# First attention's queries and output in three tiles per four heads, and the background dequantisation ending where the second layer's attention begins

## The reference

```
_L0_xattn(latents, context):             # H, KV, HD = 16, 4, 96; G = H // KV = 4 heads per key/value head
    hidden = concatenate([context, latents], axis=1)          # 64 + 256 keys
    q = (latents @ Wq.T)                                      # 16 heads of 96
    k, v = hidden @ Wk.T, hidden @ Wv.T                       # 4 heads of 96
    scores = einsum('bkgqd,bksd->bkgqs', q, k) / sqrt(96)
    out = einsum('bkgqs,bksd->bkgqd', softmax(scores), v)
    return out.reshape(b, q_len, H * HD) @ Wo.T

_L3_ffn(x, w1, w2, w3):                  # each weight is first rounded to a 16-value code
    absmax = max(abs(flat.reshape(-1, 64)), axis=1)
    dq = CODE[searchsorted(bounds, flat / absmax)] * absmax
    return (silu(x @ dq1.T) * (x @ dq2.T)) @ dq3.T

x = x + _L0_xattn(_layernorm(x), ctx, ...);  x = x + _L0_ffn(...)      # layer 0
x = x + _L1_xattn(_layernorm(x), ctx);       x = x + _L1_ffn(...)      # layer 1
x = x + _L2_xattn(...);                      x = x + _L2_ffn(...)      # layer 2
x = x + _L3_xattn(...);                      x = x + _L3_ffn(_layernorm(x), L3_w1, L3_w2, L3_w3)
```

## Time and profile before

| what | value |
|---|---|
| times of the three runs | 1754.61, 1754.72, 1748.97 us, median 1754.61 |
| the profiled execution: its time, its span | 1750.64 us, 1748.9 us |
| PE, DVE, ACT, POOL busy | 1451.7, 1115.7, 461.4, 312.8 us |
| mean granted TensorE clock | 0.884 of full |
| layer 0's attention (first transposes of the probabilities to last `pv0`) | 68 to 616 us |
| its feed-forward | to 873 us |
| layer 1; layer 2 up to `gate2` | to 1047 us; to 1139 us |

### The profile page before, as it was taken

How to read it: one execution, slowest core, us unless ns; L and a number is a source line. 1 busy time by engine, 2 the same in 40 slices (tenths; PEclk the granted TensorE clock), 3 DMA queues, 4 the chain that set the end, 5 groups by cost and what they waited for, 6 DMA issues and landing times.

```text
span 1748.9 us, 19188 instructions
## 1 busy us (share of the span) xinstructions
PE 1451.7 (83%) x6585; PEld 1150.0 (66%) x6585; DVE 1115.7 (64%) x2569; ACT 461.4 (26%) x994; POOL 312.8 (18%) x186
## 2 busy tenths in 40 slices
PE   6559999998999889898377878589997566589998
PEld 5347776685776668686266767487886355477786
DVE  4567777768777658767967556634466788854142
ACT  3214423423334323232212113113213222122010
POOL 4101211211112112111121013116422421012120
PEclk9779999999999999899655897569998788799999
DMA  6421331322223221321011013001111000001011
GB/s 202 139 69 51 89 88 49 93 77 64 77 67 84 64 62 42 84 82 41 24 43 40 23 49 91 17 1 36 46 52 49 25 1 1 1 24 61 13 38 48
DMA packets 99409, 96.42 MB, mean 55 GB/s; under 512 B 13138, under 2 KB 72418, under 8 KB 99314
## 3 DMA queue, kind: packets, MB, share of 16 engines
q1 hardware_dynamic: 98802, 94.35, 18.3%
q0 software_dynamic: 512, 0.85, 0.2%
HBM read 84.34 MB, written 10.82 MB: 54 GB/s over the span
## 4 chain that ended last, share of the span: by engine, by line
PE 62%; DVE 26%; ACT 4%; issue 4%; DMA 2%; SPq 1%; POOL 1%; ACTq 0%; DVEq 0%; POOLq 0%
PE bank L1651 49%; PE bank L1991 5%; PE bank L1743 4%; DVE nf_y L1595 3%; DVE st L1136 2%; DVE xn L1154 1%; PE bank L1676 1%; DVE mx L1504 1%; DVE xT L1113 1%; DVE e L1518 1%; PE bank L1733 1%; DVE sm L1516 1%; DVE mx L1187 1%; PE bank L1947 1%; DMA nf_a<-in_L_w 1%
## 5 line engine op out<-in xcount | busy, mean ns | idle before, releaser
L1651 PE MATMUL bank<-xT,slots 128*128 128x512 f32 (+1 forms) x1920 | 471.2, 404 | 10.4 <-DVE xT L1113 6.9
L1651 PEld LDWEIGHTS bank<-xT,slots 128*128 128x128 f32 (+1 forms) x1920 | 357.1, 187 | 110.9 <-issue 10.2
L808 POOL TENSOR_TENSOR slots<-staging,slots 128x1024 fp32r<-128x1024 f32 (+4 forms) x97 | 230.2, 2376 | 1107.0 <-ACT slots L896 1106.9
L1595 DVE TENSOR_SCALAR nf_y<-nf_w 128x512 fp32r<-128x512 f32 (+2 forms) x495 | 233.6, 499 | 25.7 <-PE bank L1991 24.7
L1651 PE MATMUL bank<-slots,h 128*128 128x512 f32 (+1 forms) x728 | 181.7, 410 | 20.1 <-DVE h L1243 13.9
L1651 PEld LDWEIGHTS bank<-slots,h 128*128 128x128 f32 (+1 forms) x728 | 142.9, 197 | 56.8 <-DVE h L1243 14.8
L1991 PE MATMUL bank<-nf_y,nf_d 128*128 128x512 f32 (+2 forms) x495 | 169.7, 427 | 10.7 <-DVE nf_y L1595 8.5
L896 ACT ACTIVATE slots<-staging 128x1024 fp32r<-128x1024 f32 (+4 forms) x97 | 98.2, 1018 | 189.9 <-PE bank L1651 173.6
L929 ACT ACTIVATE e<-bank,mx 128x320 f32<-128x320 f32 x128 | 66.4, 524 | 272.2 <-DVE mx L1190 268.1
L1209 DVE TENSOR_TENSOR x<-bank,x 128x512 f32<-128x512 f32 x72 | 49.7, 690 | 125.7 <-PE bank L1651 125.6
L1991 PEld LDWEIGHTS bank<-nf_y,nf_d 128*128 128x128 f32 (+1 forms) x495 | 94.9, 197 | 46.9 <-issue 15.6
(11 more groups left out here) (244 smaller groups left out, 1905.0 us busy)
## 6 DMA issues: line engine op xcount, KB each, us to landing
staging<-in_L_wqkT SPq DMA_DIRECT2D x16, 480.0 KB, 3.7
nf_out<-nf_w SPq DMA_DIRECT2D x30, 256.0 KB, 2.1
staging<-nf_out SPq DMA_DIRECT2D x30, 256.0 KB, 2.8
staging<-in_L_woT SPq DMA_DIRECT2D x16, 384.0 KB, 3.3
staging<-in_L_w SPq DMA_DIRECT2D x12, 512.0 KB, 3.9
nf_a<-nf_max SPq DMA_DIRECT2D x40, 128.0 KB, 3.5
nf_r<-nf_rcp SPq DMA_DIRECT2D x40, 128.0 KB, 3.4
nf_w<-in_L_w SPq DMA_DIRECT2D x15, 256.0 KB, 4.2
```

What stands on the lines that cost most here:

```text
L808: g.tensor_tensor(lo, split_source(i), hi.bitcast(FP32), ALU.subtract).then_inc(*sig.mark("weight_low", i))
L1595: v.tensor_scalar(nf_y[0:rows, i % STAIR_RING, 0:size], w_, bound, first, compare, ALU.mult)\
L1651: ins = mm(dst, l_, r_, start=i == 0, stop=i == len(passes) - 1)
```

## The change

`q0` of a stage is made in three tiles of 128 columns in place of four of 96. Tile j holds head j in rows 0 to 95 and a third of the fourth head in rows 96 to 127; the query weights are laid out for that on the host. ACT and DVE copy each tile in two pieces: head j in place, and the 32 rows of the fourth head to rows 32j of the fourth column block (`spare(j)`), where `scores0` reads it as before. `pv0` of the first three heads is unchanged. That of the fourth writes three pieces of 32 rows back to rows 96 to 127 of the three tiles. So `o0` contracts three full tiles of 128 rows, with Wo's rows in that order, in 9 matmuls. Its second weight chunk is half as long. WEIGHT of `q0` goes from 2.6 to 3.5, with three steps in place of four. BACKGROUND_END moves from `gate2` to `scores1`: all of the dequantisation lies in layer 0.

```diff
-BACKGROUND_END = "gate2"
+BACKGROUND_END = "scores1"
...
+QT0, SPARE0 = HPG * HD0 // P, P - HD0
+def spare(j):
+    return slice(j * SPARE0, (j + 1) * SPARE0)
...
-                steps += [("q0", s + 1, h) for h in ((0, 1), (2,), (3,))[j - 5]]
+                steps.append(("q0", s + 1, j - 5))
...
-WEIGHT = {"v0": 1.9, "k0": 2.6, "kc0": .7, "q0": 2.6, "scores0": .9, ...
+WEIGHT = {"v0": 1.9, "k0": 2.6, "kc0": .7, "q0": 3.5, "scores0": .9, ...
...
-        q0 = sb("q0", [HD0, 2, 2, HPG, HALF], F32R, s0)
+        q0 = sb("q0", [P, 2, 2, HPG, HALF], F32R, s0)
...
+            for i, n in enumerate((2, 1)):
+                rows = a["L0_woT"][(s % G0 * QT0 + 2 * i) * P:(s % G0 * QT0 + 2 * i + n) * P]
+                chunk(("o0", s, i), P, (n, D), [((slice(None),), rows.rearrange("(h p) n -> p h n", p=P))])
... ScalarE
-            def q0_(s, h):
-                high("q0", (s, h), q0[:, s % 2, 0, h], psum(("q0", s, h))[0:HD0])
+            def q0_(s, j):
+                bank = psum(("q0", s, j))
+                act.wait_ge(*sig.when("q0_product", (s, j)))
+                sc.activation(q0[0:HD0, s % 2, 0, j], bank[0:HD0], ACT.Copy)
+                sc.activation(q0[spare(j), s % 2, 0, QT0], bank[HD0:P], ACT.Copy).then_inc(*sig.mark("q0_high", (s, j)))
...
-                high("pv0", n, q0[:, s % 2, 0, h, bl * S:(bl + 1) * S], psum(("pv0", n))[0:HD0, 0:S])
+                if h < QT0:
+                    high("pv0", n, q0[0:HD0, s % 2, 0, h, cs], bank[0:HD0, 0:S])
+                    return
+                act.wait_ge(*sig.when("pv0_product", n))
+                for j in range(QT0):
+                    ins = sc.activation(q0[HD0:P, s % 2, 0, j, cs], bank[spare(j), 0:S], ACT.Copy)
+                ins.then_inc(*sig.mark("pv0_high", n))
... VectorE
-                low("q0", (s, h), q0[:, s % 2, 1, h], psum(("q0", s, h))[0:HD0], q0[:, s % 2, 0, h])
+                dve.wait_ge(*sig.when("q0_high", (s, j)))
+                v.tensor_tensor(q0[0:HD0, s % 2, 1, j], bank[0:HD0], q0[0:HD0, s % 2, 0, j].bitcast(FP32), ALU.subtract)
+                low("q0", (s, j), q0[spare(j), s % 2, 1, QT0], bank[HD0:P], q0[spare(j), s % 2, 0, QT0])
...
+                dve.wait_ge(*sig.when("pv0_high", n))
+                for j in range(QT0):
+                    ins = v.tensor_tensor(q0[HD0:P, s % 2, 1, j, cs], bank[spare(j), 0:S],
+                                          q0[HD0:P, s % 2, 0, j, cs].bitcast(FP32), ALU.subtract)
+                ins.then_inc(*sig.mark("pv0_low", n))
... TensorE
-                qk(s, ("q0_product", (s, h)), h * HD0, (h + 1) * HD0, lambda k: xt(k, hf * HALF, (hf + 1) * HALF), bank[0:HD0])
+                qk(s, ("q0_product", (s, j)), j * P, (j + 1) * P, lambda k: xt(k, hf * HALF, (hf + 1) * HALF), bank[:])
...
-                pe.wait_ge(*sig.when("q0_low", (s, h)))
+                pe.wait_ge(*sig.when("q0_low", (s, min(h, QT0 - 1))))
...
-                pairs = [([q0[:, s % 2, p, h, i * P:(i + 1) * P] for p in range(2)], [w[h // 2][p][:, h % 2] for p in range(2)])
-                         for h in range(HPG)]
+                pairs = [([q0[:, s % 2, p, j, i * P:(i + 1) * P] for p in range(2)], [w[j // 2][p][:, j % 2] for p in range(2)])
+                         for j in range(QT0)]
```

More of the change, by code:

```diff
@@ L109, in schedule @@
     steps += [("v0", 0, i) for i in range(TPH + BPH)]
-    steps += [("k0", 0), ("kc0", 0)] + [("q0", 0, h) for h in range(HPG)]
+    steps += [("k0", 0), ("kc0", 0)] + [("q0", 0, j) for j in range(QT0)]
     units = [(s, bl, h) for s in range(2 * G0) for h in range(HPG) for bl in range(BPH)]
@@ L235, in schedule @@
     return steps
-WEIGHT = {"v0": 1.9, "k0": 2.6, "kc0": .7, "q0": 2.6, "scores0": .9, "turn0": .4, "pv0": 1, "o0": 2.6, "up0": 2.6,
+WEIGHT = {"v0": 1.9, "k0": 2.6, "kc0": .7, "q0": 3.5, "scores0": .9, "turn0": .4, "pv0": 1, "o0": 2.6, "up0": 2.6,
           "down0": 4.8, "scores1": 2, "pv1": 1.6, "route1": 1, "z1": 2.6, "zt1": .5, "b1": 2.6, "k2": 1.3, "m2": 1.3,
@@ L493, in o0_chunks @@
         def o0_chunks(s):
-            for i in range(2):
-                rows = a["L0_woT"][(s % G0 * HPG + 2 * i) * HD0:(s % G0 * HPG + 2 * i + 2) * HD0]
-                chunk(("o0", s, i), HD0, (2, D), [((slice(None),), rows.rearrange("(h p) n -> p h n", p=HD0))])
+            for i, n in enumerate((2, 1)):
+                rows = a["L0_woT"][(s % G0 * QT0 + 2 * i) * P:(s % G0 * QT0 + 2 * i + n) * P]
+                chunk(("o0", s, i), P, (n, D), [((slice(None),), rows.rearrange("(h p) n -> p h n", p=P))])
         v0_chunks(0)
@@ L942, in pv0 @@
             def pv0(n, s, bl, h):
-                high("pv0", n, q0[:, s % 2, 0, h, bl * S:(bl + 1) * S], psum(("pv0", n))[0:HD0, 0:S])
+                cs, bank = slice(bl * S, (bl + 1) * S), psum(("pv0", n))
+                if h < QT0:
[5 more added lines that the diff above has]
+                ins.then_inc(*sig.mark("pv0_high", n))
             def up0(f, hf):
@@ L1200, in pv0 @@
             def pv0(n, s, bl, h):
-                cs = slice(bl * S, (bl + 1) * S)
-                low("pv0", n, q0[:, s % 2, 1, h, cs], psum(("pv0", n))[0:HD0, 0:S], q0[:, s % 2, 0, h, cs])
+                cs, bank = slice(bl * S, (bl + 1) * S), psum(("pv0", n))
+                if h < QT0:
+                    low("pv0", n, q0[0:HD0, s % 2, 1, h, cs], bank[0:HD0, 0:S], q0[0:HD0, s % 2, 0, h, cs])
+                    return
+                dve.wait_ge(*sig.when("pv0_high", n))
[3 more added lines that the diff above has]
+                ins.then_inc(*sig.mark("pv0_low", n))
             def add_to_x(stage, key, t, src, name=None, mark=None, scale=None):
@@ L1710, in kc0_, with q0_ @@
                    lambda k: [ctxT[:, q, k, hf * n:(hf + 1) * n] for q in range(2)], bank[0:HD0, 0:n])
-            def q0_(s, h):
+            def q0_(s, j):
                 hf = s // G0
-                bank = claim(("q0", s, h), ("q0_low", (s, h)))
-                qk(s, ("q0_product", (s, h)), h * HD0, (h + 1) * HD0, lambda k: xt(k, hf * HALF, (hf + 1) * HALF), bank[0:HD0])
+                bank = claim(("q0", s, j), ("q0_low", (s, j)))
+                qk(s, ("q0_product", (s, j)), j * P, (j + 1) * P, lambda k: xt(k, hf * HALF, (hf + 1) * HALF), bank[:])
             def scores0(n, s, bl, h):
-                pe.wait_ge(*sig.when("q0_low", (s, h)))
+                pe.wait_ge(*sig.when("q0_low", (s, min(h, QT0 - 1))))
                 pe.wait_ge(*sig.when("k0_low", s))
@@ L1722, in scores0 @@
                     bank = claim(("scores0", n, i), ("exp0", (n, i)))
-                    l_ = [q0[:, s % 2, p, h, bl * S + i * P:bl * S + (i + 1) * P] for p in range(2)]
+                    l_ = [q0[0:HD0, s % 2, p, h, bl * S + i * P:bl * S + (i + 1) * P] for p in range(2)]
                     product(bank[:, 0:KEYS0], [(l_, [k0[:, s % 2, p, bl] for p in range(2)])])\
@@ L2032, in lay_out @@
     rows = [((c * HPC + h) // REP3) * HD3 + j for c in range(KT) for h in range(HPC) for j in range(HD3)]
+    tiles = np.array([[h * HD0 + d for d in range(HD0)] + [QT0 * HD0 + h * SPARE0 + d for d in range(SPARE0)]
+                      for h in range(QT0)]).reshape(-1)
+    heads = np.concatenate([g * HPG * HD0 + tiles for g in range(G0)])
     return {
@@ L2036, in lay_out @@
         "ctxT": t(d["ctx_4096"].reshape(B * CTX, D).T),
-        "L0_wqkT": t(np.stack([np.concatenate([wq[g * HPG * HD0:(g + 1) * HPG * HD0], wk[g * HD0:(g + 1) * HD0]]).T
+        "L0_wqkT": t(np.stack([np.concatenate([wq[g * HPG * HD0 + tiles], wk[g * HD0:(g + 1) * HD0]]).T
                                for g in range(G0)])),
         "L0_wvT": t(d["L0_xattn_Wv"].T),
-        "L0_woT": t(d["L0_xattn_Wo"].T),
+        "L0_woT": t(d["L0_xattn_Wo"].T[heads]),
         "L0_wgT": t(d["L0_ffn_w_gate"].T), "L0_wuT": t(d["L0_ffn_w_up"].T), "L0_wdT": t(d["L0_ffn_w_down"].T),
```

## The result

The changed kernel takes 1779.5 us (median of 4 runs, 1777.4 to 1780.7), the kernel before 1754.7 (4 runs, 1749.0 to 1759.4): ratio 1.014, 95% interval 1.011 to 1.017. It is slower by 25 us. Its profiled span is 1775.6 us against 1748.9.

The account below looks back on a forecast made before the run. PE was taken to bound the attention, and neither PE nor DVE to fill layers 1 and 2. Attention -12, feed-forward +9, layers 1 and 2 -28 sum to -31 on 1750.6 us: 1719.5, median forecast 1720, range 1692 to 1748.

Parts of the forecast that it names:

- I take +17 us: Attention: PE's idle time grows by 17 us, from half of the late items' 30 us and the fourth heads' pieces.
- -28.9 of PE work: Attention: removed `q0` and `o0` matmuls, 22.3 us each, less 15.7 us for 67 added sums, net -28.9 us.
- the items' 30 us: Attention: nine m = 2 items each late by 3 to 4 us more, some 30 us of DVE, half under queued products.
- a few tenths for each fourth head: Attention: a few tenths of a us of PE idle time for each of 16 fourth heads.
- forecast 44.6: PE products: 8 `q0` products removed, 22.3 us, and 96 matmuls of `o0`, 22.3 us.
- +65 forecast: Attention: DVE's work grows by 65 us: `q0` subtractions 10.9, `pv0` pieces 13.5, 67 dequantisation steps 40.7.
- up to 9 us of shorter locks: `o0`'s half-length second chunk shortens POOL's lock on DVE; up to 9 us come back, left out of the sum.
- +9 forecast: Feed-forward: 3.3 us for 14 more sums and 6 us for a late m = 2 item, together +9 us.
- -28 forecast: Layers 1 and 2: all 81 dequantisation steps leave, 35 us of the chain; four fifths taken, -28 us.
- Rival (d): Layers 1 and 2: without filler sums PE's clock stays at its lower level, +30 us, 1750, no change; chance 0.09.
- Rival (c): Attention: DVE becomes the bound, unit 9.5 us instead of 8.57, +60 there, +41 in all, 1792; chance 0.07.
- (b): Attention: idle time grows by the whole 29 us and eats the gain; -12 in all, about 1739; chance 0.14.

Follow-up runs that it names:

- e6: The changed kernel with an m = 2 item's maxima and reciprocals loaded by one DMA each instead of ten (wrong rows): 1755.9 us, ratio 1.0018.
- e5: e1 from the third stage on without the fourth head's query copies and with one of its three output pieces: 1737.8 us, ratio 0.9911.
- e9: e6 from the third stage on without the fourth head's query copies and two of its three output pieces: 1720.5 us, ratio 0.9841.
- e13: e10 from the third stage on without DVE's 32-row query pieces and two of its three output pieces, ACT's kept: 1732.5 us, ratio 0.9891.
- e14: e10 with ACT's pieces left out in the same places as DVE's in e13, and DVE's kept: 1730.4 us, ratio 0.9879.
- e10: The changed kernel with right tables in 11 DMA issues per m = 2 item instead of 21, and sums five steps behind: 1741.8 us, ratio 0.9953.
- e1: The changed kernel with the dequantisation again spread up to `gate2` (tiles alone): 1759.1 us, ratio 1.0049.
- e7: e2 with its m = 2 items loaded by 3 DMAs instead of 21 (wrong rows): 1750.6 us, ratio 0.9990.
- e12: The kernel before with dequantisation ending at `scores1`, 11 DMA issues per m = 2 item and sums five steps behind: 1748.6 us, ratio 0.9989.
- e15: e10 with only the queries in three tiles, the outputs in four heads as before: 1761.6 us, ratio 1.0051.
- e16: e10 with only the outputs in three tiles, the queries in four heads as before: 1742.3 us, ratio 0.9939.
- e2: The kernel before with only the dequantisation's end moved to `scores1`: 1791.7 us, ratio 1.0231.
- e17: e15 without ACT's and DVE's 32-row pieces of the queries from the third stage on: 1748.7 us, ratio 0.9986.

## Why the prediction was wrong

The step that failed is "I take +17 us" for the growth of PE's idle time in the attention, with the -28.9 of PE work beside it. Their sum, -12, came out as +51.

- **Idle time.** +49 instead of +17. The mechanisms named (ACT ahead of DVE, late m = 2 items, waits of 3 to 7 us) were the right ones; the runs price the items at 24 us in after (e6) and the pieces at 21 to 35 (e5, e9), with what the clock adds to both. I had spread the items' 30 us over PE's queue by half, and given the pieces a few tenths for each fourth head. I also gave ACT's 21.5 us no term but those tenths, and asked only whether DVE's sum passes PE's. It didn't, and each us on ACT or DVE still cost 0.4 to 0.8 us (e13 and e14 against e10, e5 against e1, e9 against e6).
- **PE work.** -28.9 was forecast, +2.8 measured. The products gave 40.4 us in a stretch that holds 39.1 of the forecast 44.6, so that price was right. The sums cost 31.5 instead of 15.7: 0.235 us is a sum in a run of six, while over the attention they average 0.336 before and 0.361 after. Another 12 us are mostly untouched forms that ran slower at a mean clock of 0.91 instead of 0.95, a term that the sum did not have. The tiles alone bring that clock too (e1), and cheaper loads give a part of it back (e6, e7).
- **DVE's work.** +65 forecast, +46.5 measured. A 32-row piece costs what a 96-row one does (below), as taken. The added steps were cheaper: POOL is busy 9.1 us less in the attention, and a step lasts 506 ns in the mean against 530, 180 to 600 us:
```profile
L1621 DVE TENSOR_SCALAR nf_y<-nf_w 128x512 fp32r<-128x512 f32 x295 | 139.5, 506 | 3.6 <-PE bank L2017 2.4
```
   That is the term left out, up to 9 us of shorter locks. The Trainium skill (SBUF — State Buffer, "Who interferes with whom") says that DVE in its 2-port modes and GpSimd block each other for a whole instruction. The rows agree, and the packings one by one show that the shorter chunk goes with it. These are the same steps, 180 to 600 us, in e12 (no packing), e15 (queries, full chunk) and e16 (outputs, shorter chunk):
```profile
L1596 DVE TENSOR_SCALAR nf_y<-nf_w 128x512 fp32r<-128x512 f32 x313 | 155.3, 528 | 10.4 <-PE bank L1992 9.7
```
```profile
L1622 DVE TENSOR_SCALAR nf_y<-nf_w 128x512 fp32r<-128x512 f32 x304 | 148.8, 522 | 11.4 <-PE bank L2018 10.4
```
```profile
L1616 DVE TENSOR_SCALAR nf_y<-nf_w 128x512 fp32r<-128x512 f32 x320 | 152.4, 509 | 5.3 <-PE bank L2012 4.1
```
- **Feed-forward.** +9 forecast, +7 measured. e6 with its cheap loads is 5 us shorter there, near the 6 that were put for the late item.
- **Layers 1 and 2.** -28 forecast, -29 measured, clock 0.68, forecast "near 0.70". Rival (d) did not happen there: of the 35 us that the steps held of the chain, 29 came back. e2 and e7 won back 28 and 27 us there too.
- **The rivals.** Rival (c) put the unit at 9.5 us and the whole at 1792; the unit came to 9.77. But its mechanism is not what happened: it has DVE as the bound, and DVE was busy 308.7 of 420 us, as before. Engines that wait for each other gave the length that a full one would have. (b) was the gain given back; it was given back with more.
- **What the forecast time needs.** e9 came to 1720.5, the forecast to half a us, but not by its terms: the attention +1 instead of -12, the feed-forward 0 instead of +9, layers 1 and 2 -28, and 3.5 less behind them. That agreement is luck. The tiles' gain there just pays for the 65 steps moved in, which alone lengthen the attention by 23 us in e7 (0.35 each) and bring back 27 in layers 1 and 2: the move was worth next to nothing even with cheap loads.

What stays open: why queries' tiles gain nothing without their pieces (e17), and why the tiles alone lower the clock of the attention to 0.91 (e1), which only 24 us more of idle time go with.

## What to carry to other kernels

When work moves from the engine that bounds to others that feed it step by step, add it along the relay (copy, subtraction, step, sum), not engine by engine: room in the totals is no cover. Before packing steps more densely, look at the longest transfer chain between two of them and at how long its issue takes on its queue; here an edit of three lines that halves the issues was worth 26 us, as much as the change had lost. Price a filler instruction by its mean in the stretch where it will stand, not by the best run of it.

## What the runs showed of the hardware

Copies and subtractions by form in after (min/median/max ns):
```profile
L892 ACT ACTIVATE q<-bank x72: 364/374/598, 87.2 to 1563.2; 96x256 fp32r<-96x256 f32 x48, 128x256 fp32r<-128x256 f32 x16, 128x512 fp32r<-128x512 f32 x8
L959 ACT ACTIVATE q<-bank x48: 371/372/375, 149.5 to 668.2; 32x256 fp32r<-32x256 f32 x48
L1226 DVE TENSOR_TENSOR q<-bank,q x48: 416/420/425, 150.7 to 669.5; 32x256 fp32r<-32x256 f32 x48
L930 ACT ACTIVATE q<-bank x24: 588/594/597, 38.8 to 596.6; 96x512 fp32r<-96x512 f32 x24
L931 ACT ACTIVATE q<-bank x24: 589/592/594, 39.4 to 597.3; 32x512 fp32r<-32x512 f32 x24
```
32 rows cost what 96 do: 0.372 against 0.375 us for 256 columns on ACT, 0.420 against 0.421 on DVE, and 0.592 against 0.594 for 512 columns on ACT. Ten DMA issues of a queue took 5.85 us, 0.58 each (e2's queue above); e6 and e7 moved the same bytes in one issue and took that away. And a gap of PE cost beyond itself: in e2 a product of 12 matmuls took 4.42 us at a granted clock of 0.61 behind 3.2 us of gaps, against 2.79.
